# Attention passes: an order of its own for VectorE and TensorE in the last rounds of a pass

## The reference

```python
# network 1, two layers, 4 heads of 64
z = (x @ W).reshape(n, HEADS, ODIM)
e = leaky_relu(el[src] + er[dst], 0.2)
ex = exp(e - segment_max(e, dst)[dst])
out = segment_sum(z[src] * (ex / segment_sum(ex, dst)[dst])[:, :, None], dst)
# network 2, three layers, 8 heads of 32
scores = sum(Q[dst] * kt, -1) / sqrt(HD) * mu[l].T[edge_type]   # kt: K[src] through W_E[edge_type]
w = softmax of scores over the edges of one dst
agg = segment_sum(V[src] * w[..., None], dst)
```

## Time and profile before

| | |
|---|---|
| median of 3 runs | 7132.12 us (7111.1 to 7143.51) |
| profiled execution | 7125.7 us, span 7124.0 |
| VectorE busy | 3946.7 us, 55% |
| TensorE matmuls, weight loads busy | 4450.9 us, 62%; 3312.9 us, 47% |
| ScalarE, GpSimd busy | 3581.0 us, 50%; 3726.1 us, 52% |
| VectorE adds L1043, 1576 | 668.9 us, mean 424 ns |
| VectorE products L1035, 481 of 128x1024 | 583.4 us, mean 1214 ns |
| granted TensorE clock, mean | 0.75 |

### The profile page before, as it was taken

How to read it: one execution, slowest core, us unless ns; L and a number is a source line. 1 busy time by engine, 2 the same in 40 slices (tenths; PEclk the granted TensorE clock), 3 DMA queues, 4 the chain that set the end, 5 groups by cost and what they waited for, 6 DMA issues and landing times. The chain is left out here.

```text
span 7124.0 us, 82903 instructions
## 1 busy us (share of the span) xinstructions
PE 4450.9 (62%) x21728; PEld 3312.9 (47%) x21728; DVE 3946.7 (55%) x9715; ACT 3581.0 (50%) x9073; POOL 3726.1 (52%) x3967
## 2 busy tenths in 40 slices
PE   4544354545667366755667895677795667795444
PEld 3443233323444233444555694555694545683332
DVE  7222222245667366675878545778544877673223
ACT  3333132234444344455656575666575666565554
POOL 0666566646662666425666225666234666225664
PEclk6555566666667676787888897888897888896666
DMA  1111233333441344336666226666325666433332
GB/s 59 52 50 46 65 98 93 93 93 106 113 113 59 112 113 111 88 114 201 195 196 192 87 83 186 195 194 194 98 80 176 194 197 191 125 107 114 93 91 87
DMA packets 395664, 864.27 MB, mean 121 GB/s; under 512 B 93353, under 2 KB 203851, under 8 KB 391763
## 3 DMA queue, kind: packets, MB, share of 16 engines
q0 software_dynamic: 209680, 608.73, 30.5%
q1 hardware_dynamic: 177296, 246.02, 10.5%
q10 hardware_dynamic: 8243, 4.30, 0.2%
HBM read 743.33 MB, written 115.44 MB: 121 GB/s over the span
## 5 line engine op out<-in xcount | busy, mean ns | idle before, releaser
L769 POOL DMA_INDIRECT ring<-tab_kv,idx_i x1044 | 988.4, 947 | 644.4 <-issue 291.0
L769 POOL DMA_INDIRECT ring<-tab_z,src_i x880 | 835.6, 950 | 501.5 <-issue 251.2
L845 PE MATMUL pp<-ring,scratch 128*128 128x264 f32 x1760 | 786.1, 580 | 424.7 <-DVE acc L1043 227.1
L1218 PE MATMUL pp<-ring,oh 128*128 128x256 f32 x1760 | 603.9, 496 | 641.7 <-issue 301.5
L788 PE MATMUL pq<-Qs,oht 128*128 x4176 | 679.5, 310 | 467.2 <-DVE X L955 245.6
L1043 DVE TENSOR_TENSOR acc<-acc,pp 128x264 f32 x1576 | 668.9, 424 | 377.9 <-PE pp L845 98.9
L1352 DVE TENSOR_TENSOR acc<-acc,pp 128x256 f32 x880 | 370.4, 421 | 890.1 <-DMA tab_z<-zs 272.0
L875 ACT ACTIVATE oht<-oht,part_c 128x1024 bf16<-128x1024 bf16 x284 | 325.2, 1145 | 1008.3 <-DMA oht<-lo_row_p 563.2
L1218 PEld LDWEIGHTS pp<-ring,oh 128*128 128x128 f32 x1760 | 408.3, 248 | 837.7 <-issue 730.1
L788 PEld LDWEIGHTS pq<-Qs,oht 128*128 128x128 bf16 x4176 | 436.5, 109 | 687.6 <-issue 560.7
L845 PE MATMUL pp<-ring,X 128*128 128x264 f32 x2088 | 653.5, 443 | 148.9 <-DVE acc L1043 55.1
(11 more groups left out here) (361 smaller groups left out, 9110.8 us busy)
## 6 DMA issues: line engine op xcount, KB each, us to landing
oht<-lo_row_p SPq DMA_DIRECT2D x174, 256.0 KB
oht<-lo_row_s SPq DMA_DIRECT2D x110, 256.0 KB
drow<-in_dst SPq DMA_DIRECT2D x25, 1024.0 KB
tab_h<-hs SPq DMA_DIRECT2D x25, 1024.0 KB, 4.4
tab_kv<-X SPq DMA_DIRECT2D x50, 396.0 KB, 2.7
tab_kv<-X SPq DMA_DIRECT2D x50, 384.0 KB, 3.4
ring<-tab_kv,idx_i POOLq DMA_INDIRECT x1044
ring<-tab_z,src_i POOLq DMA_INDIRECT x880
```

The source lines that it names most:

```text
L769: nc.gpsimd.indirect_dma_start(out=one(w, c, 0, row), out_offset=None, in_=table, in_offset=bass.IndirectOffsetOnAxis(ap=idx[:, w * WC + c ...
L845: last = nc.tensor.matmul(pp[(w * NU + n) % NB][:, 0:W8], oh[:, w % 2, UC * n + c, :], one(w, UC * n + c, 0, W8), start=(c == 0), stop=(c ...
L1218: last = nc.tensor.matmul(bank[:, c * D:(c + 1) * D], oh[:, b, 2 * k + c, :], ring[:, b, k, c, :], start=True, stop=True)
```

## The change

Four new order strings, and the code that picks them. In round `r` = `nw` TensorE takes `LAST_T` in both kinds of pass, and VectorE `LAST_V_DOTS` or `LAST_V_SUMS`. In round `nw` - 1 of a sums pass VectorE takes `SOON_V_SUMS`, which differs from the usual order in the place of `L`. No instruction is added, removed or altered in size; DMAs, GpSimd and ScalarE are as before.

```diff
--- before.py
+++ after.py
@@ -678,6 +678,11 @@
     ORDER_T_DOTS = order("l G0 C1 h3 G1 h4 G2 h5 h6 G3 h7 G4 C3 C4 G5 C5 n0 G6 n1 G7 n2")
     ORDER_T_SUMS = order("l G0 C1 G1 Q0 Q1 G2 Q2 Q3 G3 G4 C3 G5 C4 C5 G6 G7")
 
+    LAST_V_DOTS = order("D1 W0 P6 P7 D2 W1 t W2 W3 D3 A0 A1 A2 A3 A4 A5")
+    LAST_V_SUMS = order("D1 W0 P12 P13 D2 W1 P14 P15 W2 W3 t D3 A0 A1 A2 A3 A4 A5 A6 A7 A8 A9 A10 A11")
+    SOON_V_SUMS = order("W0 P12 P13 W1 P14 P15 W2 t D1 A0 A1 D2 A2 W3 A3 D3 L A4 A5 B A6 A7 A8 A9 A10 A11")
+    LAST_T = order("C1 G0 G1 C3 C4 C5 G2 G3 G4 G5 G6 G7")
+
     def attend(Qs, heads, row, at_k, idx, table, scratch, lay, plus=None):
         dots = heads == HD
         nw, pen, link, lo_s, lo_row = lay.nw, lay.pen, lay.link, lay.lo, lay.lo_row
@@ -851,7 +856,7 @@
                     for q in range(NQ):
                         qrows(0, tl, q)
                     for r in range(nw + 2):
-                        for kind, p in order_t:
+                        for kind, p in (LAST_T if r == nw else order_t):
                             if kind == "l" and r + 1 < nw:
                                 tn = tiles(r + 1)
                             elif kind == "Q" and 0 < r < nw and p < quads(r):
@@ -1047,7 +1052,13 @@
 
                     for r in range(nw + 2):
                         b = r - 2
-                        for kind, p in order_v:
+                        if r == nw:
+                            now = LAST_V_DOTS if dots else LAST_V_SUMS
+                        elif r == nw - 1 and not dots:
+                            now = SOON_V_SUMS
+                        else:
+                            now = order_v
+                        for kind, p in now:
                             if kind == "s" and r < nw:
                                 dot(r, p)
                             elif kind == "R" and r < nw:
```

## The result

Over 9 runs of each kernel the changed one takes 7160.44 us (7141.84 to 7167.44), the kernel before 7127.73 (7111.1 to 7145.04). The ratio is 1.0038, 95% interval 1.0028 to 1.0049: 27 us slower, between 20 and 35; the two medians lie 33 us apart. The change lies within the half per cent that was forecast as most likely. The profiled execution took 7167.03 us, span 7165.2, clock 0.75.

The account below looks back on a forecast made before the run. The prediction took VectorE, almost solid at the five pass ends, as the bound; two sums passes at +3.8 and three dots at +3.7 gave about +19 us, 7151 us from the 7132.12 median, range 7120 to 7180, chance 0.60.

Parts of the forecast that it names:

- the half per cent that was forecast as most likely: Total within 0.5%, 36 us, of the kernel before: chance 0.80, against 0.15 for slower and 0.05 for faster.
- VectorE sets the pace at a pass end, its work is kept, so only waits count: Pass ends: VectorE almost solid over 21.5 us in the third pass, its work kept instruction for instruction.
- The bound: Pass ends: an order wins at most VectorE's waits for TensorE, 1.9 us first pass, 1.2 third, 3.8 fifth.
- D1 at the head: Closing round on VectorE: D1 first waits for C1, 1.2 us in dots passes, 3.1 us idle in sums passes.
- The wait behind C3: Closing round: units queued behind C3 and C5 make VectorE's adds wait 1.4 us in dots, 0.9 in sums passes.
- Sum: Pass ends: two sums passes at +3.8 us and three dots passes at +3.7 give 18.7, say +19 us.
- The clock: Rival at the pass ends: clock falls at C3, 11.5 us more, 30 in all, 7162 us; chance 0.22.
- The bounds of +7 and +6.3: Upper bounds per pass: dots +7 us with both waits and a slower clock, sums +6.3 with lower clock throughout.
- Faster, or nothing at all: Two rivals: VectorE's waits vanish, 10 us less, 7122 us, chance 0.10; no effect, 7132 us, chance 0.08.
- The early `L`: Sums passes, third round from the end: VectorE's sum unchanged, C3, C5 and last units up to 1.22 us later.
- The round before it 4 us longer: Sign in the trace after: round before last 4 us longer, last scan to last sum no longer than now.
- Two signs that it would be wrong: Pass ends: D1 starts without a wait, or C3 (L817) comes earlier after the round's start than now.

Follow-up runs that it names:

- e8: Kernel before with replayed orders in the last two rounds of both pass kinds, closing sums and products interleaved, C3, C4, C5 late: ratio 1.0003.
- e1: The changed kernel again, no edit, on a chip where the kernel before takes 6151.12 us: ratio 1.0040, 25 us slower than before.
- e2: The changed kernel with the closing-round orders in the three dots passes only, sums passes as before: ratio 1.0036 to the kernel before, 22 us.
- e5: The changed kernel with C3 and C4 moved behind G4 and C5 behind G5 on TensorE, VectorE's orders kept: ratio 1.0016 to the kernel before, 11 us.
- e7: The changed kernel with unread matmuls in TensorE's pauses, six ahead of G0 and twelve ahead of C3: ratio 1.0024 to the kernel before, 17 us.
- e4: Kernel before with only the early L in the third round from the end of the sums passes: ratio 0.9995.
- e9: e5 with the first product ahead of D1 on VectorE in both orders: ratio 1.0018 to the kernel before.
- e6: Kernel before with only TensorE's closing-round order LAST_T, VectorE's orders as before: ratio 1.0041, 29 us.

## Why the prediction was right, and where its sizes were off

- *VectorE sets the pace at a pass end, its work is kept, so only waits count.* Right. The sum from D1 to the scores was 8.2 and is 8.2. No instruction of VectorE became longer, and e8, which takes the waits away as far as I found, wins 0.6 us in a dots close and nothing in the total. The bound was drawn too tight, though: VectorE is idle for 2.75 us in the third close and 10.0 in the first, and its adds' waits for TensorE are 1.2 and 3.7 of that (the earlier trace rows start only at the round before last). Most of the rest are 0.21 us for every add behind an add, and those an order can change too.
- *D1 at the head.* Forecast a wait of 1.2 us in the dots passes; measured 0.15 (third), 1.0 (fourth) and 0.15 (fifth). The forecast was read from a pass whose round before had run at the lower clock (0.66 in the earlier trace rows), and the edit has nothing to do with that. Where the granted clock was 1.00 over the last 8 us ahead of the close (a stretch chosen here), ScalarE's copy ended 0.66 before the last add ahead of D1 began, as here (3976.69 against 3977.35), and D1 waited 0.15; where it was lower the copy ended 0.1 to 0.95 behind that point, as in the earlier trace rows, and D1 waited 0.5 to 1.0. This holds for the dots closes of the change, e1, e2, e5 and e7. In the sums passes 3.1 was forecast; it is 0.5 and 2.8, and 3.2 and 2.6 in e1.
- *The wait behind C3.* This is the term that was mis-sized: 1.4 forecast in the dots passes, 3.48 measured in the third; 0.9 in the sums passes, 3.95 measured. In the third pass the first unit of G behind C5 began 2.2 us after the scores, not 1.5, and its sum could be added 4.5 after them, not 2.6; the three adds behind it came 1.8, 1.5 and 0.9 us apart and not 0.85. The lower clock of that stretch (0.59; 0.50 in the first pass) goes with it: e7, which keeps it away for longer, waits 1.94 and 1.35 in these two places.
- *Sum.* A dots close grew by 6.0 in the third and fourth pass where 3.7 was forecast, and only 1.6 in the fifth, whose close before already had a low clock. The sums closes grew 3.9 and 5.5, for 3.8. (Besides the two that were read there are three other pass ends, not four; the sum counts five.) In all 3.9 + 5.5 + 6.0 + 6.0 + 1.6 = 23, for 19. That the total came so near is partly luck: D1's wait was 1 too large in two of the dots passes, the wait behind C3 1.4 to 3 too small, and the fifth pass had its low clock before the edit as well.
- *The clock.* The rival came true as a mechanism, with a price close to the one it named (the total is +27, it said +30), and the forecast should have given it more than 0.22. I argued from pauses in the trace of before that leave the clock at 1.00; the new order has two pauses, 2.13 and 2.63, in one round with 8 matmuls between them. In the third pass the first of them, with 0.72 of standing ahead of C1, was enough to bring a spell before C3 was reached. That the third pass of before showed a low clock only beside a pause of 5.71 was no ground to call shorter ones harmless; the fifth, whose 0.87 stands in the earlier trace rows, fell to 0.50 at 6136.37 behind pauses of 1.34 and 1.78. The pause at C3 was also shorter than forecast (2.6 to 3.6, not 4.5), in part because G0 and G1 ran at 0.50 themselves and took 3.52 us, not 2.05. e7 shows the link with the pauses from the other side: with matmuls in them the clock of the third pass is 1.00 up to the first unit behind C5. The bounds of +7 and +6.3 need the time of a unit at the lower clock, and no row shows it. In the third pass the 16 records of four units took 6.29 us, 1.57 a unit, most of them at 0.50; at 1.00 they took 3.72, 0.93 a unit.
- *Faster, or nothing at all.* Neither: the interval excludes both. VectorE's waits did not vanish; those of its adds for TensorE grew from 98.9 to 124.7 over the program.
- *The early `L`.* Forecast: no cost on VectorE, but later C3 and D1, 3.1 us in all. e4 shows no cost alone, but D1 does not stand first there. How much of D1's wait in the sums passes (0.5 to 3.2) the early `L` makes is open.
- *Signs.* "The round before it 4 us longer" was 6.3 (17.7 from 3977.35 to 3995.07; 11.4 before), the last round 0.3 shorter. Two signs that it would be wrong came true in part. D1 waited only 0.15 in the third and fifth pass, and C3 (L817, now L822) came earlier after the round's start there: 8.48 us, where it was 8.92. The scores came 0.44 earlier in these two passes and 1.5 in the first, 0.4 and 0.8 later in the fourth and second. All five closes grew all the same, so the earlier scores bought nothing; the step from them to the adds is where the time went.

What stays open: what C1 and D1 at the head cost through TensorE's pauses (e9 didn't separate it), and why spells at the lower clock vary between runs of one kernel, as in the fifth pass of the two traces of before (24.7 and 21.8).

## What to carry to other kernels

At the end of a pipeline find the engine that is solid; an order can win only that engine's idle time, and here its waits for TensorE were 1 to 4 us a pass. Before taking a wait from one trace, look at the granted clock ahead of it: here the wait of 1.2 us was read from a pass with a clock of 0.66 ahead of its end, and it was 0.15 where the clock was 1.00. Moving a chain forward pays only if something waits for its result, and nothing did here. Don't put a step that waits for a long chain (C3) ahead of work of the same engine that is ready (G2 to G7): TensorE stood 2.63 us at C3 with those units behind it in the third pass, and the clock was 0.50 from 3986.48 to 3993.31, in just the stretch that had to catch up.

## What was not expected of the hardware

**The clock fell on pauses of 2 to 3 us.** In the third pass it fell during the first of them (2.13 us) and again behind the second (2.63); in the first pass during one of 3.33. The units of the sum then ran at 0.59 and 0.50 of full; 16 records took 6.29 us in the third pass, and 3.94 in its last round at 1.00. Matmuls in the pauses (six in 1.46 us, twelve in 2.75) kept it at 1.00 up to their end in four of the five passes. Pauses alone do not foretell it: the third and fifth pass of before have nearly the same ones (0.97 and 1.79; 1.34 and 1.78), and only the fifth has a spell behind them.

**The same program differs by 15% between chips.** The kernel before took 6151.12 on chip 14 and 7072 to 7074 on chip 12; the first runs, whose chip is not on record, took 7127.73, and 7160.44 with the change. The gathers cost the same each, and the time between them does not (busy us, mean ns, idle before, what ended it). First the changed kernel's first profile, then e1:

```profile
L774 POOL DMA_INDIRECT ring<-tab_kv,idx_i x1044 | 988.1, 946 | 645.0 <-issue 288.1
```

```profile
L774 POOL DMA_INDIRECT ring<-tab_kv,idx_i x1044 | 992.9, 951 | 364.4 <-issue 290.6 <-POOLq L150 47.3 <-PE pp L850 14.0
```

On the slower chip some gathers come after a pause of 3 us, as the second here; on the faster one they go on in steps of 1.25 us. An idle of over 2.5 us stands ahead of 94 of the 1044 gathers of this line in the first trace, and ahead of 3 in e1:

```profile
3702.32 0.94 POOL L774 DMA_INDIRECT ring<-tab_kv,idx_i  x1 [0.30 <-issue]
3706.59 0.94 POOL L774 DMA_INDIRECT ring<-tab_kv,idx_i  x1 [3.33 <-remote]
```

Over all 3572 gathers GpSimd is idle 2136 us before them in the first of these traces and 1238 in e1: 897 of the 985 us between their spans. It is 2074 in e6 on chip 12. What causes these pauses was not tried; the price of the edit, at the pass ends, was the same 25 and 27 us on both.
